# All of V' as rows in fp32r one period ahead, laid out anew through device memory

## The chip, the cores and the metric

One core of one Trainium2 chip runs the kernel. The metric is the device time of one execution in microseconds (us), the median of several. TensorE is called PE, VectorE DVE, ScalarE ACT, GpSimd POOL and SyncE SP, as the profile does.

## The reference

A block of cross attention and a quantised feed-forward layer over 128 samples of 64 positions and 128 features, with 16 heads:

```python
x = x + attention(layernorm(x), ctx_1024, ctx_1024, Wq, Wk, Wv, Wo, bo, mask)   # causal, dots * 64 ** -0.5
x = x + ffn(layernorm(x), w_gate, w_up, w_down)
# attention: softmax(q k^T) v over 16 heads of 64, then out @ Wo + bo
# ffn: bitlinear(silu(bitlinear(x, w_gate)) * bitlinear(x, w_up), w_down)
# bitlinear: activations rounded to 8 bits per row, weights to -1, 0, 1 times their mean size
```

## The kernel before

The samples go in 16 groups of eight, each group in two quads of four samples, so there are 32 quads. In the setup the kernel folds the weights: M = Wq Wk^T per head and N = Wv Wo per head, so that K' = ctx M and V' = ctx N come straight from the context, and the products of probabilities and V', summed over the heads, are the attention's output. A loop over 34 periods does in period n: the scores of quad n (`scores`, L411 for the later rows of the samples and L419 for the earlier ones), the product of quad n-1 (`attend`, L433 and L437, with V' in the tile `vp`), the transposes of the quantised x of quad n-1 (`transpose_xq`, L460), gate and up of quad n-1 (`gate_up`, L473, L476), down of quad n-2 (`down`, L446), and the transposes of the probabilities of quad n in three parts (`prob_transposes`, L489). A period with an even n also sums the next group's context on DVE (`sum_ctx`, L720), one with an odd n rounds and splits the one after it on ACT and POOL.

Between these stand units of work that depend on nothing late, each filling one PSUM bank of 128x512, four banks in turn: eight units of K' for the next group (`k_unit`, L294 to L296: three fp32r products of a high and a low part), four units of V' for the 32 later keys of each sample of quad n (`v_tiles`, L305: sixteen fp32 products into 32 partitions each, straight in the layout that `attend` wants, here called tile units), and four units of V' for the earlier keys of quad n+1 (`v_row_unit`, L313 to L315: three fp32r products with the samples' positions on all 128 partitions, here called row units). ACT copies every bank out (L540, with `take_v`, `take_key`, `take_rows`). The row units' copies lie in four tiles `v_rows` in a layout that `attend` can't use; SP moves each with four DMAs of 64 KB, 32 partitions to 32 partitions, into `vp` in the next period (`move_rows`, L235): 16 moves per quad.

The order on each engine is written out by hand, and semaphores are waited for at fixed counts. On PE a period reads: scores, attend, four tile units, four K' units, transposes of x, one K' unit, the late keys' mean (L454), down, gate and up, two K' units, probabilities' part 0, one K' unit, gate and up, part 1, four row units, part 2. DVE's order is: shift the scores by their bias (L779) and take row maxima, add the residual of quad n-1 and its statistics, quantise x (L840), then sum the exponentials and invert them (L801), then the feed-forward steps. POOL subtracts the row maxima (L978, L981), takes the roots (L922), and later multiplies the probabilities by the inverse sums (L990 in two halves, L992). The first half of L990 releases part 0 of `prob_transposes`.

Of the kernel before, what the change touches and what calls it, by code (L numbers as in the profile page):

```python
# [37 lines left out]
def build(nc, x, x_t, ctx_t, mask, wq, wk, wv, wo, bo, ffn_w, ident, causal, out):  # L42
# [14 lines left out]
    with ExitStack() as es:  # L57
# [21 lines left out]
        n_w = sb("n_w", [P, 2, HP, D])  # L79
# [30 lines left out]
        v_rows = [sb(f"v_rows{i}", [P, QB, D]) for i in range(QB)]  # L110
# [31 lines left out]

# [9 lines left out]
        m_ready, m_hi_done, m_lo_done, n_ready, n_done, n_hi_done, n_lo_done = (sem(n) for n in (  # L152
            "m_ready", "m_hi_done", "m_lo_done", "n_ready", "n_done", "n_hi_done", "n_lo_done"))
# [3 lines left out]
        k_ready, v_ready, scores_ready = (sem(n) for n in ("k_ready", "v_ready", "scores_ready"))  # L157
# [6 lines left out]
        vp_moved = [sem(f"vp_moved{i}") for i in range(QB)]  # L164

        cthi_ready, k_evac, v_evac, pt_evac, xqt_evac, exp_done, tanh_done = (sem(n) for n in (
            "cthi_ready", "k_evac", "v_evac", "pt_evac", "xqt_evac", "exp_done", "tanh_done"))
# [12 lines left out]
        V_UNITS, K_UNITS = QB, 8  # L180
# [3 lines left out]
        makes_k = lambda n: live(n) and n // 2 + 1 < GROUPS  # L184

# [6 lines left out]
        def _(sp):  # L192
# [25 lines left out]
            def load_ctx(g):  # L218

                sp.wait_ge(latesum_done, g - 1)  # L220
                sp.wait_ge(v_ready, V_UNITS * 2 * (g - 1))
                sp.dma_start(ct[g % 2][:], ctx_t[g]).then_inc(ctx_loaded[g % 2], 16)
# [6 lines left out]
            def move_rows(n, h4):  # L229

                if n:
                    sp.wait_ge(attn_ready, n)
                sp.wait_ge(rows_evac, QB * n + h4 + 1)
                for b in range(QB):
                    sp.dma_start(vp[h4 * R:(h4 + 1) * R, b, 0, :, :],  # L235
                                 v_rows[h4][b * R:(b + 1) * R, :, :]).then_inc(vp_moved[h4], 16)

            for n in PERIODS:
                g, r = n // 2, n % 2
                if live(n, 2):  # L240
                    for c in range(2):

                        sp.wait_ge(hb_ready, 2 * (n - 2) + c + 1)
                        if live(n, 3):
                            sp.wait_ge(down_ready, n - 2)
                        sp.dma_start_transpose(hid_t[:, c, :, :], hid_b[:, c, :]).then_inc(ht_moved, 16)
                if live(n):
                    move_rows(n, 0)
                    if r == 1 and g + 2 < GROUPS:
                        load_ctx(g + 2)  # L250
                    for h4 in range(1, QB):
                        move_rows(n, h4)
                if live(n) and r == 1 and g + 2 < GROUPS:
                    load_xt(g + 2)
                if live(n, 2):
                    store(n - 2)
                if makes_k(n) and r == 0:
                    if g:
                        sp.wait_ge(x1_done, 2 * g)
                    sp.dma_start(x_res[(g + 1) % 2][:], x[g + 1]).then_inc(xres_loaded[(g + 1) % 2], 16)  # L260
            for i in range(2):
                sp.wait_ge(stored[i], 16 * 2 * (GROUPS // 2))
# [3 lines left out]
        def _(pe):  # L266
# [34 lines left out]
            def v_tiles(n, b, dst):  # L301

                col = (n % 2 * 4 + 2) * P // 2 + b * R
                for h4 in range(QB):
                    t = mm(dst[h4 * R:(h4 + 1) * R, :], ct[n // 2 % 2][:, col:col + R], heads_of(n_w, h4),  # L305
                           start=True, stop=True)
                t.then_inc(v_ready, 1)

            def v_row_unit(n, h4, dst):

                par, cols = n // 2 % 2, slice(n % 2 * 2 * P, n % 2 * 2 * P + P)
                hi, lo = heads_of(n_hi, h4), heads_of(n_lo, h4)
# [40 lines left out]
            def fill_v(n, b):  # L353
                if not live(n):
                    return
                if b == 0:
                    pe.wait_ge(biased, 3 * n + 2)
                    pe.wait_ge(ctx_loaded[n // 2 % 2], 16 * (n // 4 + 1))
                elif b == 2:
                    pe.wait_ge(biased, 3 * n + 3)  # L360
                elif b == 3 and n:
                    pe.wait_ge(rows_evac, QB * n + 4)
                v_tiles(n, b, banks[b])

            def fill_k(n, u):
                if not makes_k(n):
                    return
                if u == 0 and n % 2 == 0:
                    pe.wait_ge(ctlo_ready, n // 2 + 2)
                if u < 4 and n == 0:  # L370
                    pe.wait_ge(rows_evac, u + 1)
                elif u < 4:
                    pe.wait_ge(v_evac, V_UNITS * n + u + 1)
                else:
                    pe.wait_ge(k_evac, H + K_UNITS * n + u - 3)
                k_unit(8 * (n % 2) + u, (n // 2 + 1) % 2, banks[u % 4])

            def fill_rows(n, h4):

                if not live(n):  # L380
                    return
                if n == 0:
                    pe.wait_ge(n_lo_done, h4 + 1)
                if n < 1:
                    pe.wait_ge(v_evac, h4 + 1)
                elif makes_k(n - 1):
                    pe.wait_ge(k_evac, H + K_UNITS * (n - 1) + h4 + 5)
                else:
                    pe.wait_ge(v_evac, V_UNITS * (n - 1) + h4 + 1)
                v_row_unit(n, h4, banks[h4])  # L390

            def scores(n):
# [4 lines left out]
                if n == 0:  # L397
                    pe.wait_ge(n_done, 4)
                else:
                    pe.wait_ge(rows_evac, QB * n + 2)  # L400
# [13 lines left out]
                if n:  # L414
                    pe.wait_ge(rows_evac, QB * n + 3)
# [7 lines left out]
            def attend(n):  # L423
                pe.wait_ge(pt_evac, 3 * n + 3)
                pe.wait_ge(v_evac, V_UNITS * n + V_UNITS)
                for h4 in range(QB):
                    pe.wait_ge(vp_moved[h4], 16 * QB * (n + 1))
# [64 lines left out]
            for n in PERIODS:  # L492
# [4 lines left out]
                fill_v(n, 0)  # L497
                fill_v(n, 1)
                fill_v(n, 2)
                fill_v(n, 3)  # L500
                if n == 0:
                    for h4 in range(QB):
                        fill_rows(0, h4)
                fill_k(n, 0)
                fill_k(n, 1)
                fill_k(n, 2)
                fill_k(n, 3)
# [4 lines left out]
                fill_k(n, 4)  # L512
# [26 lines left out]
        def _(act):  # L539
# [45 lines left out]
            def round_n(k):  # L585
                act.wait_ge(n_done, k + 1)
                part = slice(4 * (k // 2), 4 * (k // 2) + 4)
                copy(flat(n_hi[:, k % 2, part, :]), flat(n_w[:, k % 2, part, :])).then_inc(n_hi_done, 1)

            def take_v(n, b):  # L590
                if live(n):
                    act.wait_ge(v_ready, V_UNITS * n + b + 1)
                    if n:
                        act.wait_ge(attn_ready, n)
                    copy(flat(vp[:, b, 1, :, :]), banks[b]).then_inc(v_evac, 1)

            def take_key(n, u):
                if makes_k(n):
                    take_k((n // 2 + 1) % 2, 8 * (n % 2) + u, H + K_UNITS * n + u + 1, u % 4)

            def take_rows(n, h4):
                if live(n):
                    act.wait_ge(rows_ready, QB * n + h4 + 1)
                    if n:
                        act.wait_ge(vp_moved[h4], 16 * QB * n)
                    copy(flat(v_rows[h4][:, :, :]), banks[h4]).then_inc(rows_evac, 1)
# [18 lines left out]
            for n in PERIODS:  # L625
                if n == 0:
                    for k in range(4):
                        round_n(k)
# [3 lines left out]
                take_v(n, 0)  # L632
                take_v(n, 1)
                if live(n) and n:
                    exponential(n, 0)
                take_v(n, 2)
                if live(n) and n:
                    exponential(n, 1)
                take_v(n, 3)
                if n == 0:  # L640
                    for h4 in range(QB):
                        take_rows(0, h4)
                if n == 0:
                    exponential(n, 0)
                    exponential(n, 1)
                take_key(n, 0)
                take_key(n, 1)
                take_key(n, 2)
                take_key(n, 3)
# [4 lines left out]
                take_key(n, 4)  # L654
                if live(n, 1):
                    tanh(n - 1, 0)
                take_key(n, 5)
                take_key(n, 6)
                if live(n):
                    take_probs(n, 0)  # L660
                take_key(n, 7)
# [374 lines left out]
```

## Time and profile before

| | before |
|---|---|
| median of 3 runs | 706.51 us (704.72 to 708.13) |
| the profiled execution's own time | 707.55 us |
| its span in the trace | 705.7 us |
| mean granted clock of PE | 0.978 of full speed |
| busy, share of the span | PE 96%, DVE 76%, ACT 69%, POOL 50% |
| DMA engines, mean busy share of the data queue | 36.2% |
| moved by DMA | 63.31 MB, 72,922 packets |

The span is the part of the execution that the trace covers; the profiled execution took 1.85 us more than it. PE's matmuls are pipelined and their ends are modelled, so a row's length overlaps the next row; the distance from one start to another start is what a stretch of PE costs. In a timeline, several like instructions are merged into a row with their count (x8), and an idle time before a row stands in brackets with what ended it. Every fp32 product counts as two instructions in the trace.

### The profile page before, as it was taken

What the parts mean: (1) busy time and instruction counts of PE and PEld (TensorE: products, weight loads), DVE (VectorE), ACT (ScalarE), POOL (GpSimd) and SP (SyncE); (2) the same over time, 40 slices, a digit from 0 to 9 for tenths busy, and PEclk for the clock granted to TensorE, in tenths of its full rate; (3) what the DMA queues carried; (4) which work ended last, traced back from release to release, by engine and by line L of the source; (5) the groups of instructions that cost most, each with busy time, mean ns of one, the idle gap of its engine ahead of it and who ended that gap; (6) DMA issues with size and microseconds to landing.
All of it is one profiled execution on the core that took longest, in us unless ns stands there. A gap on an engine that the chain in (4) does not pass through costs nothing.

```text
span 705.7 us, 19010 instructions
## 1 busy us (share of the span) xinstructions
PE 675.8 (96%) x7258; PEld 452.9 (64%) x7258; DVE 535.7 (76%) x1398; ACT 487.6 (69%) x862; POOL 352.2 (50%) x359
## 2 busy tenths in 40 slices
PE   8999999999999999999999999999999999998852
PEld 5576766667766666676766667666666766665531
DVE  5667878778787877877878777787877777888663
ACT  5768767776886777678766767876676678665521
POOL 0536455464545546455554655555455545554531
PEclk9999999999999999999999999999999999999975
DMA  7023433333333434333433334353333434332231
GB/s 263 3 75 90 99 91 85 94 91 80 103 94 93 94 88 89 84 99 90 114 74 96 85 87 94 87 114 85 90 91 77 101 87 105 99 72 66 61 69 30
DMA packets 72922, 63.31 MB, mean 90 GB/s; under 512 B 44672, under 2 KB 49024, under 8 KB 72832
## 3 DMA queue, kind: packets, MB, share of 16 engines
q1 hardware_dynamic: 72832, 62.09, 36.2%
q8 instruction: 58, 0.95, 0.6%
q14 instruction: 32, 0.26, 0.1%
HBM read 15.91 MB, written 4.19 MB: 28 GB/s over the span
## 4 chain that ended last, share of the span: by engine, by line
PE 91%; issue 3%; POOL 2%; DVE 2%; DMA 1%; ACT 0%; POOLq 0%; SPq 0%; DVEq 0%
PE ps_up L411 8%; PE ps_up L305 7%; PE ps_a L433 7%; PE ps_b L489 6%; PE ps_up L294 5%; PE ps_up L295 4%; PE ps_up L296 4%; PE ps_low L305 4%; PE ps_kv L305 4%; PE ps_a L437 4%; PE ps_low L419 4%; PE ps_up L313 2%; PE ps_up L314 2%; PE ps_up L315 2%; PE ps_kv L294 2%
## 5 line engine op out<-in xcount | busy, mean ns | idle before, releaser
L540 ACT ACTIVATE vp<-ps_up 128x512 f32<-128x512 f32 x64 | 38.2, 597 | 143.1 <-PE ps_up L305 143.1
L990 POOL TENSOR_TENSOR prob_up<-prob_up,row_rec 128x512 f32<-128x512 f32 x64 | 65.9, 1051 | 129.6 <-DVE row_rec L801 129.6
L975 POOL TENSOR_TENSOR hid_b<-hid,neg_round 128x512 bf16<-128x512 f32 x64 | 65.2, 1039 | 105.9 <-ACT hid L540 105.9
L978 POOL TENSOR_TENSOR prob_up<-prob_up,row_max 128x1024 f32<-128x1024 f32 x32 | 61.2, 1913 | 62.7 <-DVE row_max L786 62.7
L848 DVE SCALAR_TENSOR_TENSOR gated<-gated,ps_g 128x512 f32<-128x512 f32 x64 | 44.0, 688 | 58.3 <-ACT gated L619 57.3
L779 DVE SCALAR_TENSOR_TENSOR prob_up<-ps_up,rs,bias_up 128x512 f32<-128x512 f32 x64 | 45.1, 748 | 48.4 <-PE ps_up L411 48.4
L540 ACT ACTIVATE kp<-ps_up 128x512 f32<-128x512 f32 x120 | 68.7, 605 | 8.9 <-PE ps_up L296 7.4
L433 PEld LDWEIGHTS ps_a<-vp,prob_t 128*32 128x32 f32 x2048 | 57.8, 111 | 19.7 <-issue 18.5
L433 PE MATMUL ps_a<-vp,prob_t 128*32 128x128 f32 x2048 | 62.6, 275 | 0.7 <-ACT prob_t L540 0.7
L540 ACT ACTIVATE prob_t<-ps_b 128x512 f32<-128x512 f32 x96 | 57.1, 594 | 7.7 <-PE ps_b L489 7.7
L411 PE MATMUL ps_up<-kp,xt 128*32 128x256 f32 (+1 forms) x768 | 61.9, 454 | 0.0
L305 PE MATMUL ps_up<-n_w,ct 128*32 128x512 f32 x512 | 60.8, 592 | 0.8 <-DVE prob_up L779 0.8
L294 PE MATMUL ps_up<-ct_hi,m_hi 128*128 128x512 f32 x120 | 58.7, 489 | 0.0
L922 POOL TENSOR_TENSOR rs<-ve,neg_half 128x2 f32<-128x2 f32 x64 | 44.4, 708 | 16.9 <-DVE ve L716 14.8
L619 ACT ACTIVATE gated<-ps_g,g_half 128x512 f32<-128x512 f32 x64 | 44.0, 687 | 11.6 <-PE ps_g L473 11.6
L295 PE MATMUL ps_up<-ct_lo,m_hi 128*128 128x512 f32 x120 | 47.5, 396 | 0.0
L296 PE MATMUL ps_up<-ct_hi,m_lo 128*128 128x512 f32 x120 | 47.5, 396 | 0.0
L853 DVE TENSOR_TENSOR hid<-gated,ps_u 128x512 f32<-128x512 f32 x64 | 44.0, 687 | 2.2
L540 ACT ACTIVATE hid<-hid,qs 128x512 f32<-128x512 f32 x64 | 42.7, 715 | 3.9 <-DVE qs L867 3.9
L489 PE MATMUL ps_b<-id_sb,prob_up 128*128 128x128 f32 x256 | 40.0, 280 | 4.1 <-POOL prob_up L990 3.8
L489 PEld LDWEIGHTS ps_b<-id_sb,prob_up 128*128 128x128 f32 x256 | 32.2, 143 | 16.9 <-POOL prob_up L990 5.9
L294 PEld LDWEIGHTS ps_up<-ct_hi,m_hi 128*128 128x128 f32 x120 | 22.6, 189 | 29.2 <-issue 24.3
(186 smaller groups left out, 1797.9 us busy)
## 6 DMA issues: line engine op xcount, KB each, us to landing
vp<-v_rows SPq DMA_DIRECT2D x512, 64.0 KB, 2.0
ct<-in_ctx_t SPq DMA_DIRECT2D x16, 256.0 KB, 2.8
x_res<-in_x SPq DMA_DIRECT2D x16, 256.0 KB, 2.8
xt<-in_x_t SPq DMA_DIRECT2D x16, 256.0 KB, 3.2
out<-x SPq DMA_DIRECT2D x32, 128.0 KB, 2.0
hid_t<-hid_b SPq DMA_TRANSPOSE x64, 2.7
kp<-in_wk SPq DMA_DIRECT2D x2, 256.0 KB, 3.7
kp<-in_wq SPq DMA_DIRECT2D x2, 256.0 KB, 4.4
```

The costliest lines, as they stand in the source:

```text
L294: mm(dst, hi, ct_hi[par][:], start=True, stop=False)
L295: mm(dst, hi, ct_lo[par][:], start=False, stop=False)
L296: mm(dst, lo, ct_hi[par][:], start=False, stop=True).then_inc(k_ready, 1)
L305: t = mm(dst[h4 * R:(h4 + 1) * R, :], ct[n // 2 % 2][:, col:col + R], heads_of(n_w, h4), start=True, stop=True)
L411: t = mm(ps_up[r * R:(r + 1) * R, col:col + w * R], xt[par][:, rows], kp[par][:, c * w:(c + 1) * w, key:key + R], start=True, stop=True)
L433: t = mm(ps_a[r * R:(r + 1) * R, 0:D], prob_t[:, a, r * R:(r + 1) * R], vp[:, r, a // QB, a % QB, :], start=(a == 0), stop=(a == HP - 1))
L489: t = nc.tensor.transpose(ps_b[:, k * P:(k + 1) * P], flat[:, k * P:(k + 1) * P], id_sb[:])
L540: copy = lambda dst, src, **kw: nc.scalar.activation(dst, src, ACT.Copy, **kw)
L779: v.scalar_tensor_tensor(prob_up[:, c, :, :], banks[c].rearrange("p (h j) -> p h j", j=R), rs1[:, 0:1], bias_up[:, n:n + 1, c * R:(c + 1) ...
L975: p.tensor_tensor(hid_b[:, c, :], hid[:, c, :], neg_round[:].broadcast_to([P, F]), ALU.add).then_inc(hb_ready, 1)
L978: p.tensor_tensor(prob_up[:], prob_up[:], row_max[0][:].rearrange("p (c h o) -> p c h o", c=1, o=1) .broadcast_to([P, 2, H, R]), ALU.subtr ...
L990: p.tensor_tensor(prob_up[:, half, :, :], prob_up[:, half, :, :], rows(row_rec[:, 0, :], H, R), ALU.mult).then_inc(normed, 1)
```

## The change

Nothing is left of the tile units: all of V' (both halves of the keys) is computed by row units, eight per quad, all in the period before the quad's own. N is then kept only as a high and a low part: ACT writes the high part from PSUM at once, and the low part is made by DVE from PSUM (`n_low`), where POOL made it from a copy (`split_n`). A device-memory tensor `v_mem` with room for two quads takes the rows: SP writes each of the eight `v_rows` tiles to it as one DMA of 256 KB (`save_row`), and in the quad's own period, after `attend` of the quad before, reads four pieces of 512 KB into `vp` (`load_v`), 32 partitions each, with 4 KB in a piece. `attend` waits for these four (`vp_loaded`). The table FILL sets in which of a period's 16 slots a row unit (o) or a K' unit (k) stands. Slots 0 to 6 come before the transposes of x, 7 after them, 8 and 9 before part 0 of the probabilities, 10 after it, and 11 to 15 between part 1 and part 2. Period 0 has eight more for quad 0.

```diff
-        n_w = sb("n_w", [P, 2, HP, D])
-        v_rows = [sb(f"v_rows{i}", [P, QB, D]) for i in range(QB)]
+        v_rows = [sb(f"v_rows{i}", [P, QB, D]) for i in range(2 * QB)]
...
+        FILL = "o0 o1 o2 o3 k0 k1 o4 k2 o5 k3 o6 k4 o7 k5 k6 k7"
+        FIRST_FILL = [("v", 0, u) for u in range(V_UNITS)]
+        def fills(n):
+            own = FIRST_FILL if n == 0 else []
+            if makes_k(n):
+                return own + [("kv"[c == "o"], n + (c == "o"), int(u)) for c, u in (w for w in FILL.split())]
+            return own + [("v", n + 1, u) for u in range(V_UNITS) if live(n + 1)]
...
-            def move_rows(n, h4):
+            def save_row(n, u):
+                jh, h4 = u // QB, u % QB
+                if n >= 2:
+                    sp.wait_ge(vp_loaded, 16 * QB * (n - 1))
+                sp.wait_ge(rows_evac, V_UNITS * n + u + 1)
+                sp.dma_start(v_mem[n % 2, h4, :, jh, :], v_rows[u][:, :, :].rearrange("p a e -> p (a e)")).then_inc(rows_saved[u], 16)
+            def load_v(n):
                 if n:
                     sp.wait_ge(attn_ready, n)
-                sp.wait_ge(rows_evac, QB * n + h4 + 1)
-                for b in range(QB):
-                    sp.dma_start(vp[h4 * R:(h4 + 1) * R, b, 0, :, :],
-                                 v_rows[h4][b * R:(b + 1) * R, :, :]).then_inc(vp_moved[h4], 16)
+                for h4 in range(QB):
+                    for jh in range(2):
+                        sp.wait_ge(rows_saved[jh * QB + h4], 16 * (n + 1))
+                    sp.dma_start(vp[h4 * R:(h4 + 1) * R, :, :, :, :].rearrange("p b c a e -> p b (c a e)"),
+                                 v_mem[n % 2, h4, :, :, :].rearrange("(b j) c x -> j b (c x)", j=R)).then_inc(vp_loaded, 16)
...
             def attend(n):
                 pe.wait_ge(pt_evac, 3 * n + 3)
-                pe.wait_ge(v_evac, V_UNITS * n + V_UNITS)
-                for h4 in range(QB):
-                    pe.wait_ge(vp_moved[h4], 16 * QB * (n + 1))
+                pe.wait_ge(vp_loaded, 16 * QB * (n + 1))
...
-                fill_v(n, 0)
-                fill_v(n, 1)
-                fill_v(n, 2)
-                fill_v(n, 3)
-                fill_k(n, 0)
-                fill_k(n, 1)
-                fill_k(n, 2)
-                fill_k(n, 3)
+                for i in range(0, 7):
+                    fill(n, i)
...
                     transpose_xq(n - 1)
-                fill_k(n, 4)
+                fill(n, 7)
...
-                fill_k(n, 5)
-                fill_k(n, 6)
+                for i in range(8, 10):
+                    fill(n, i)
                 if live(n):
                     prob_transposes(n, 0)
-                fill_k(n, 7)
+                fill(n, 10)
...
                     prob_transposes(n, 1)
-                fill_rows(n + 1, 0)
-                fill_rows(n + 1, 1)
-                fill_rows(n + 1, 2)
-                fill_rows(n + 1, 3)
+                for i in range(11, 16):
+                    fill(n, i)
                 if live(n):
                     prob_transposes(n, 2)
...
             def take_n(k):
-                copy(flat(n_w[:, k % 2, 4 * (k // 2):4 * (k // 2) + 4, :]), banks[N_BANK[k]]).then_inc(n_done, 1)
+                copy(flat(n_hi[:, k % 2, 4 * (k // 2):4 * (k // 2) + 4, :]), banks[N_BANK[k]]).then_inc(n_hi_done, 1)
...
+            def n_low(k):
+                dve.wait_ge(n_hi_done, k + 1)
+                half = slice(4 * (k // 2), 4 * (k // 2) + 4)
+                low_part(n_lo[:, k % 2, half, :], banks[N_BANK[k]], n_hi[:, k % 2, half, :], 1.0, n_lo_done)
```

The scores of quad 0 then wait for all four low parts (`n_lo_done`), since those read the banks that the scores overwrite.

PE in a period of the middle, just before and after the transposes of x (L460 before, L459 now). Before, the last K' unit ahead of them is the eighth unit after `attend`:

```order
L296 MATMUL ps_low<-ct_hi,m_lo 128x512
L294 MATMUL ps_kv<-ct_hi,m_hi 128x512
L295 MATMUL ps_kv<-ct_lo,m_hi 128x512
L296 MATMUL ps_kv<-ct_hi,m_lo 128x512
L460 MATMUL ps_a<-id_sb,xq 128x128 x2
L294 MATMUL ps_up<-ct_hi,m_hi 128x512
```

Now (row units at L332 to L334, K' units at L320 to L322):

```order
L332 MATMUL ps_low<-n_hi,ct_hi 128x512
L333 MATMUL ps_low<-n_hi,ct_lo 128x512
L334 MATMUL ps_low<-n_lo,ct_hi 128x512
L459 MATMUL ps_a<-id_sb,xq 128x128 x2
L320 MATMUL ps_kv<-ct_hi,m_hi 128x512
```

The unit for bank ps_kv, which stood ahead of the transposes, now stands behind them, and every later unit has moved back by one place: one more of them follows part 1 of the probabilities.

SP in two periods of the middle, an even one and the odd one after it. Before:

```order
L246 DMA_TRANSPOSE hid_t<-hid_b 128x4x128 x2
L235 DMA vp<-v_rows 32x512 x16
L227 DMA out<-x_0 128x256
L260 DMA x_res<-in_x 128x512
L246 DMA_TRANSPOSE hid_t<-hid_b 128x4x128 x2
L235 DMA vp<-v_rows 32x512 x4
L222 DMA ct<-in_ctx_t 128x512
L235 DMA vp<-v_rows 32x512 x12
L216 DMA xt<-in_x_t 128x512
L227 DMA out<-x_0 128x256
```

Now:

```order
L265 DMA_TRANSPOSE hid_t<-hid_b 128x4x128 x2
L254 DMA vp<-v_mem 32x4x1024 x4
L274 DMA x_res<-in_x 128x512
L232 DMA ct<-in_ctx_t 128x512
L245 DMA v_mem<-v_rows 128x512 x4
L237 DMA out<-x_0 128x256
L245 DMA v_mem<-v_rows 128x512 x4
L265 DMA_TRANSPOSE hid_t<-hid_b 128x4x128 x2
L254 DMA vp<-v_mem 32x4x1024 x4
L226 DMA xt<-in_x_t 128x512
```

The sixteen moves have become four reads, behind the same two transposes; the eight writes stand behind the reads and the inputs' loads, four ahead of the store of `out` and four behind it.

## Rows read from the trace of the kernel before

**Rows 1.** The page, part 1: busy time of each engine, share of the span, instructions.

```profile
PE 675.8 (96%) x7258; PEld 452.9 (64%) x7258; DVE 535.7 (76%) x1398; ACT 487.6 (69%) x862; POOL 352.2 (50%) x359
```

**Rows 2.** Waits: engine, tile, line, who was waited for: us in total, times, longest.

```profile
PE ps_a L460 <- DVE xq L840: 8.1, 3, 4.1
...
PE ps_b L489 <- POOL prob_up L990: 3.8, 2, 2.2
```

**Rows 3.** Timeline of PE, period 15: start us, us, engine, line, op, out<-in, forms.

```profile
332.73 1.92 PE L411 MATMUL ps_up<-kp,xt 128*32 128x512 f32 x16
...
337.95 1.90 PE L305 MATMUL ps_up<-n_w,ct 128*32 128x512 f32 x16
...
341.50 0.50 PE L294 MATMUL ps_up<-ct_hi,m_hi 128*128 128x512 f32 x1
...
344.39 0.38 PE L460 MATMUL ps_a<-id_sb,xq 128*128 128x128 f32 x2
...
347.81 0.60 PE L489 MATMUL ps_b<-id_sb,prob_up 128*128 128x128 f32 x4
...
350.54 0.39 PE L313 MATMUL ps_up<-n_hi,ct_hi 128*128 128x512 f32 x1
...
351.23 0.39 PE L313 MATMUL ps_low<-n_hi,ct_hi 128*128 128x512 f32 x1
...
353.13 1.93 PE L411 MATMUL ps_up<-kp,xt 128*32 128x256 f32 x32
```

**Rows 4.** Timeline of PE, period 16.

```profile
368.24 0.60 PE L489 MATMUL ps_b<-id_sb,prob_up 128*128 128x128 f32 x4
...
373.54 1.92 PE L411 MATMUL ps_up<-kp,xt 128*32 128x512 f32 x16
```

**Rows 5.** Timeline of DVE and POOL, period 15.

```profile
334.80 1.41 DVE L779 SCALAR_TENSOR_TENSOR prob_up<-ps_up,rs,bias_up 128x512 f32<-128x512 f32 x2 [1.24 <-PE ps_up L411]
...
338.08 1.91 POOL L978 TENSOR_TENSOR prob_up<-prob_up,row_max 128x1024 f32<-128x1024 f32 x1 [1.78 <-DVE row_max L786]
...
343.18 0.48 DVE L840 TENSOR_SCALAR xq<-xn,qs 128x128 f32<-128x128 f32 x2
...
345.82 0.35 DVE L801 RECIPROCAL row_rec<-row_sum 128x32 f32<-128x32 f32 x1
...
346.25 2.06 POOL L990 TENSOR_TENSOR prob_up<-prob_up,row_rec 128x512 f32<-128x512 f32 x2 [3.93 <-DVE row_rec L801]
```

**Rows 6.** Timeline of DVE and POOL, period 16.

```profile
364.13 0.41 DVE L720 TENSOR_REDUCE late_sum<-ct 128x8 f32<-128x256 f32 x1
...
367.00 2.06 POOL L990 TENSOR_TENSOR prob_up<-prob_up,row_rec 128x512 f32<-128x512 f32 x2 [4.25 <-DVE row_rec L801]
```

**Rows 7.** Timeline of PE and POOL, period 30, and the start of period 31.

```profile
638.84 1.93 PE L411 MATMUL ps_up<-kp,xt 128*32 128x256 f32 x32
...
652.38 2.05 POOL L990 TENSOR_TENSOR prob_up<-prob_up,row_rec 128x512 f32<-128x512 f32 x2 [3.92 <-DVE row_rec L801]
...
653.48 0.66 PE L489 MATMUL ps_b<-id_sb,prob_up 128*128 128x128 f32 x4 [2.20 <-POOL prob_up L990]
...
660.22 1.92 PE L411 MATMUL ps_up<-kp,xt 128*32 128x512 f32 x16
```

**Rows 8.** DMA issues: out<-in, queue, count, size, median us to landing.

```profile
vp<-v_rows SPq DMA_DIRECT2D x512, 64.0 KB, 2.0
```

**Rows 9.** Windows: stretch, us, busy us of engines, PEclk, DMA share, GB/s.

```profile
353.00:373.41 20.41, 20.41 (x234) 14.08 (x232) 16.16 (x44) 14.81 (x27) 10.29 (x11) 1.00 0.37 86
...
360.20:370.00 9.80, 9.80 (x66) 6.66 (x57) 7.83 (x25) 8.85 (x16) 5.55 (x7) 1.00 0.40 100
...
11.00:14.00 3.00, 2.81 (x23) 2.43 (x24) 1.06 (x3) 2.14 (x5) 0.00 (x0) 1.00 1.03 407
```

**Rows 10.** Timeline of ACT and PE at the end of the setup.

```profile
23.82 0.61 ACT L540 ACTIVATE n_w<-ps_up 128x512 f32<-128x512 f32 x1
...
24.84 2.17 PE L411 MATMUL ps_up<-kp,xt 128*32 128x256 f32 x32
```

More of the change, by code:

```diff
@@ L246, in _ @@
                         sp.dma_start_transpose(hid_t[:, c, :, :], hid_b[:, c, :]).then_inc(ht_moved, 16)
+                if n == 0:
+                    for u in range(V_UNITS):
+                        save_row(0, u)
                 if live(n):
[L248 to L256, printed above, removed]
+                    load_v(n)
                 if makes_k(n) and r == 0:
@@ L260, in _ @@
                     sp.dma_start(x_res[(g + 1) % 2][:], x[g + 1]).then_inc(xres_loaded[(g + 1) % 2], 16)
+                if r == 1 and g + 2 < GROUPS:
+                    load_xt(g + 2)
+                elif g + 2 < GROUPS:
+                    load_ctx(g + 2)
+                if live(n + 1):
+                    for u in range(4):
+                        save_row(n + 1, u)
+                if live(n, 2):
+                    store(n - 2)
+                if live(n + 1):
+                    for u in range(4, V_UNITS):
+                        save_row(n + 1, u)
             for i in range(2):
@@ L583, in take_n_sum, with take @@
                 copy(n_sum[:], ps_a[:, 0:D], scale=1.0 / (S * R)).then_inc(nsum_done, 1)
[L585 to L606, printed above, removed]
+            def take(n, i):
+                i += len(FIRST_FILL) if n == 0 else 0
+                if i >= len(fills(n)):
+                    return
+                kind, m, u = fills(n)[i]
+                if kind == "k":
+                    take_k((m // 2 + 1) % 2, 8 * (m % 2) + u, H + K_UNITS * m + u + 1, i % 4)
+                else:
+                    act.wait_ge(rows_ready, V_UNITS * m + u + 1)
+                    if m:
+                        act.wait_ge(rows_saved[u], 16 * m)
+                    copy(flat(v_rows[u][:, :, :]), banks[i % 4]).then_inc(rows_evac, 1)
             def round_hid(n, c):
@@ L653, in _ @@
                     take_xq(n - 1)
-                take_key(n, 4)
+                take(n, 7)
                 if live(n, 1):
                     tanh(n - 1, 0)
-                take_key(n, 5)
-                take_key(n, 6)
+                for i in range(8, 10):
+                    take(n, i)
                 if live(n):
                     take_probs(n, 0)
-                take_key(n, 7)
+                take(n, 10)
                 if live(n, 1):
@@ L665, in _ @@
                     take_probs(n, 1)
-                take_rows(n + 1, 0)
+                take(n, 11)
                 if live(n) and n % 2 == 1 and n // 2 + 2 < GROUPS:
                     round_ctx(n // 2 + 2)
-                take_rows(n + 1, 1)
-                take_rows(n + 1, 2)
-                take_rows(n + 1, 3)
+                for i in range(12, 16):
+                    take(n, i)
                 if live(n):
```

134 lines of the change are left out of this document (55 added, 79 removed).

## The prediction

> **What bounds the kernel now.** I read the busy times, the waits, then two periods of the timeline engine by engine. PE is busy 96% of the span [rows 1], and nearly all its waiting is in the first and last periods: three waits for x and two for the probabilities in the whole run [rows 2]. So a period of the middle costs what PE's own instructions cost: scores start at 332.73 and again at 353.13, 20.40 us later, and 20.41 us later again [rows 3, 4]. The reader might conclude that less work on PE is time saved one for one. That holds only as long as nothing PE waits for comes after PE would get there, so the second thing to read is how early those results are.
>
> The chain that matters starts with the scores themselves. DVE shifts them from 334.80, POOL subtracts the maxima from 338.08, DVE has quantised x by 343.18 + 0.48 = 343.66, has inverted the sums at 345.82 + 0.35, and POOL multiplies the probabilities from 346.25 in two halves of 1.03 [rows 5]. Part 0 can be transposed after the first half: at 347.28, which is 14.55 us after the scores' start. PE got there at 347.81, 15.08 after it [rows 3]. In an even period DVE also sums the context (0.41) in front of this, and POOL starts at 367.00 [rows 6]: ready 368.03, which is 14.90 after the start 353.13, and PE is there at 15.11 [rows 4]. **PE's slack at part 0 is thus 0.5 us in odd and 0.2 us in even periods.** It does not show as a wait, so the list of waits hides it. Period 30 makes no K' and shows the chain laid bare: POOL's first half ends at 652.38 + 1.03 = 653.41, PE starts at 653.48, 14.64 after its scores, and had idled 2.20 us [rows 7]. A result is used 0.08 us after POOL's recorded end.
>
> **The change, part by part.** *Units on PE.* From the first tile unit to the first K' unit it is 341.50 - 337.95 = 3.55 us for four; a row unit is 351.23 - 350.54 = 0.69, a K' unit 0.70 (four of them and a start after the tiled products make 344.39 - 341.50 = 2.89) [rows 3]. PE drops out of its tiled form once per period either way, about 0.2 us in all, now straight after `attend`. Ahead of the transposes stood 3.55 + 2.89 = 6.44 us; eight units in the new form would cost 0.2 + 8 x 0.70 = 5.8. PE's own work thus shrinks by **0.62 us per period**, 20 us in all, and this is the gain that the change seems to offer.
>
> *Where the units stand.* Only seven of them are now ahead of the transposes of x, and ten ahead of part 0 where there were eleven. The work ahead of part 0 falls by 0.62 + 0.70 = 1.32 us, and the work behind it rises by 0.70. Undisturbed, PE would reach the transposes of x at 11.66 - 1.32 = 10.34 us and part 0 at 15.08 - 1.32 = 13.76 (even: 13.79). But x is ready at 10.93 at the latest (343.66), so PE stops there for about 0.5 us, and part 0 is ready at 14.55, or 14.90, whatever PE does: every link of that chain hangs on the scores or on DVE's and POOL's fixed order, none on a unit. ACT's exponentials may start some 0.1 us earlier, since the two copies before them are of faster units, but DVE sums them only after quantising x, so nothing comes of it. With 0.08 of delay and about 0.04 for a cold start, part 0 begins at 14.67 in odd periods and at 15.02 in even ones. The first stop is swallowed by the second.
>
> *Per period.* From part 0 to the next scores it was 353.13 - 347.81 = 5.32 and 373.54 - 368.24 = 5.30 [rows 3, 4]; with one unit more it is 6.02 and 6.00. An odd period takes 14.67 + 6.02 = 20.69 (**+0.29**) and an even one 15.02 + 6.00 = 21.02 (**+0.61**). Periods 1 to 29: 15 x 0.29 + 14 x 0.61 = **+12.9 us**. What was saved stands as idle time ahead of part 0, and the moved unit is paid for in full.
>
> *Period 0 and the setup.* The last of N's copies starts at 23.82 and takes 0.61 [rows 10]; two low parts must follow on DVE, 1.41 / 2 = 0.70 each by the PSUM operation of the same shape [rows 5], so the scores start at about 25.9 instead of 24.84: +1.1. V' of quad 0 costs eight row units (5.7) for four tile and four row units (6.3): -0.6. Then three units more stand ahead of part 0 and one more behind: +2.8. Sum **+3.3**. POOL loses `split_n`, which only shortens a queue that isn't waited for here.
>
> *The tail.* Period 30 had four row units behind part 1; quad 31 now has its eight before part 0, in idle time. Period 30 took 660.22 - 638.84 = 21.38 [rows 7] and loses four units: **-2.8**. Period 31 loses its tile units, but it waits for the chain as period 30 did, and the rest is untouched: 0.
>
> *ACT and PSUM.* The copies stay 16 per period of the same shape, the banks go round as before: 0.
>
> *DMA.* A move lands 2.0 us after its issue [rows 8]. The reads are issued after `attend`, at about 6.4 us of the period behind the two transposes, and are wanted 2.6 us into the next: 17 us of cover. Their rate is not in the trace. Moves to 32 partitions ran at 100 GB/s with a share of 0.40, so 250 GB/s at full share; loads to all 128 partitions reached 407 [rows 9]. By these bounds 2.1 MB take 5.2 to 8.4 us, and the same for the eight writes. I take 8.4 for the reads (same 32 partitions as the moves) and 5.2 for the writes. The engines' load per period goes from 0.37 x 20.41 = 7.6 us, less 4.2 for the moves, plus 13.6, to 17.0 of about 20.9 us; with both at 250 GB/s it is 20.2. It fits, so this term is 0; it is also the term least known. On SP sixteen issues become twelve, and what a write waits for (its copy by ACT, the earlier reads) is done before SP reaches it; behind the last write stand the next period's transposes, which have until the down product, 12 us into it.
>
> The Trainium skill (SBUF — State Buffer, "Door 1: The DMA port swizzle") speaks against these reads: a transfer into 32 partitions reaches 8 of the 16 ports, some 218 GB/s, and two transfers to different partitions don't add up. By that, as an estimate from the page, the reads take 9.6 us, 1.2 more than by the moves' rate, and the sum stays. The moves' row agrees in kind, 250 against 407 GB/s, though a bit above the page's figure.
>
> *The sum.* 12.9 + 3.3 - 2.8 = +13.4 us on the profiled execution's 707.55, which gives 721.0. That execution lay 1.04 above the median of 706.51, so for the median I say **720 us**, 1.9% slower.
>
> **The rivals.** *The gain on PE is real (faster).* If the probabilities were ready before 13.8 us, PE would never stop, each period of the middle would fall by 0.62, and the time would be 706.5 - 29 x 0.62 + 0.5 = 689 us. For it: PE is at 96%, and POOL's recorded spans are rough. Against: in period 30 PE did wait, and began at 14.64, where POOL's row says. I give it 0.05. *Half way (no change).* If part 0 is ready 0.45 us before the rows say, the sum is nil: 706 us; about 0.07, for the same roughness. (0.5%, or 3.5 us, is about what a measurement of this kernel can tell.)
>
> *DMA becomes the bound (slower still).* The decisive point is a load of 20.9 us per period. If the reads run at 220 GB/s and the writes at 250 the load is 3.4 + 9.5 + 8.4 = 21.3, plus the end of one quad's writes that the next reads must wait for (2.0), which makes the chain read, attend, read longer than the rest: at a period of 21.7 the time is 720 + 29 x 0.8 = 743 us. For it: threefold traffic, in one queue. Against: 17 us of cover. 0.10. *The change does not do what it says*, that is, the row units run slower than 0.70 because the weights are the context: row units did so already, so no chance apart.
>
> **How the numbers follow.** The forecast of the chain gets 0.78; its own range, with 0.2 us per period of error either way and 2 us for setup and tail, is 712 to 730. The range reaches up towards DMA's case and a little below: 709 to 740. Faster by over 0.5%: 0.05; within: 0.07; slower: 0.78 + 0.10 = 0.88.
>
> **What would show it.** In the changed profile, PE's waits must name DVE's xq (near 0.5 us in each period) and POOL's prob_up (some 0.3 to 0.8 us in each) where there were three and two waits; periods alternate near 20.7 and 21.0; part 0 starts 14.7 and 15.0 us after the scores; five units stand behind part 1; no wait of `attend` for `vp`. I am wrong if part 0 starts earlier than 14.5 us, if PE waits for a DMA in each period, or if ACT's copies of the units hold PE back.

## The result, and the profile after

The changed kernel takes 722.37 us (median of four runs, 720.32 to 723.01) against 707.32 for the kernel before on the same chip (four runs: the three behind the 706.51 above and one more). The ratio is 1.0214, 95% interval 1.0179 to 1.0250: slower by 2.1%, where 720 us and 1.9% were forecast. The profiled execution's span grew from 705.7 to 720.8 us.

The page of the changed kernel, parts 1, 2 and 3 in part (the busy times answer to [rows 1]; in part 2 each digit is a fortieth of the span):

```profile
PE 668.6 (93%) x6586; PEld 490.1 (68%) x6618; DVE 531.8 (74%) x1402; ACT 483.6 (67%) x858; POOL 347.6 (48%) x355
...
PEclk9999999999999999999999999999999999999955
...
q1 hardware_dynamic: 103552, 162.75, 85.2%
```

PE is busy for less time, 668.6 us for 675.8, in a longer span. The data queue moves 162.75 MB where it moved 62.09, and its share has gone from 36.2% to 85.2%.

Who waited for whom in the changed kernel (total us, times, longest):

```profile
PEld ps_a L459 <- DVE xq L825: 33.2, 32, 5.9
PEld ps_b L488 <- POOL prob_up L967: 25.4, 32, 2.0
...
PE ps_a L459 <- DVE xq L825: 19.5, 29, 5.6
PEld ps_a L432 <- issue: 18.6, 62, 0.3
...
PE ps_b L488 <- POOL prob_up L967: 9.3, 17, 1.5
```

These are the two waits that [rows 2] had three times and twice; PE's own rows now have them 29 and 17 times. PE's weight loads (PEld) meet both in all 32 periods that have them, where they met them three and four times before. No wait of `attend` for `vp` is in the list. Such a wait could stand there as "issue", with nobody named; but at the lines of `attend` the weight loads have 18.6 us of it in 62 places, and had 18.5 in 62 before.

Part 4 of the two pages, the chain of work that ended last, says the same of the whole span. Before:

```profile
PE 91%; issue 3%; POOL 2%; DVE 2%; DMA 1%; ACT 0%; POOLq 0%; SPq 0%; DVEq 0%
```

and now:

```profile
PE 39%; POOL 23%; issue 21%; DVE 16%; ACT 1%; DMA 0%; POOLq 0%; DVEq 0%; SPq 0%
```

What took the time was PE's own work for 91% of the span, and is now for 39% of it; POOL and DVE have another 39%, and DMA 0%.

Timeline of the changed kernel, PE, periods 15 and 16, at the places of [rows 3, 4]:

```profile
342.39 1.92 PE L412 MATMUL ps_up<-kp,xt 128*32 128x512 f32 x16
...
353.20 0.52 PE L459 MATMUL ps_a<-id_sb,xq 128*128 128x128 f32 x2 [0.36 <-DVE xq L825]
...
357.04 0.66 PE L488 MATMUL ps_b<-id_sb,prob_up 128*128 128x128 f32 x4
...
358.68 0.60 PE L488 MATMUL ps_b<-id_sb,prob_up 128*128 128x128 f32 x4
...
362.62 0.60 PE L488 MATMUL ps_b<-id_sb,prob_low 128*128 128x128 f32 x4
...
363.15 1.93 PE L412 MATMUL ps_up<-kp,xt 128*32 128x256 f32 x32
...
378.13 0.66 PE L488 MATMUL ps_b<-id_sb,prob_up 128*128 128x128 f32 x4 [0.44 <-POOL prob_up L967]
...
384.24 1.06 PE L412 MATMUL ps_up<-kp,xt 128*32 128x512 f32 x8
```

and POOL at the same places:

```profile
355.93 2.06 POOL L967 TENSOR_TENSOR prob_up<-prob_up,row_rec 128x512 f32<-128x512 f32 x2 [3.93 <-DVE row_rec L786]
...
377.02 2.06 POOL L967 TENSOR_TENSOR prob_up<-prob_up,row_rec 128x512 f32<-128x512 f32 x2 [4.25 <-DVE row_rec L786]
```

The odd period takes 20.76 us, the even one 21.09; both took 20.4. Part 0 begins 357.04 - 342.39 = 14.65 and 378.13 - 363.15 = 14.98 us after the scores. POOL's first half of the probabilities ends at 355.93 + 1.03 = 356.96 and 378.05, 0.08 us before PE starts on it. In the odd period PE's row names no wait; the row of its weight load does:

```profile
357.04 0.42 PEld L488 LDWEIGHTS ps_b<-id_sb,prob_up 128*128 128x128 f32 x4 [0.55 <-POOL prob_up L967]
```

POOL's instruction stands 13.54 us after the odd scores, 13.52 before [rows 5]: the chain has not moved, PE has come up against it.

### The profile page after: what moved, and what is told of

The parts are those of the page before. It is cut to its first block, busy times and chain, and to the rows that moved or that the text cites. A ratio compares the mean times of both kernels' runs of the same rounds, so it can differ in the third digit from the quotient of the medians.

```text
span 720.8 us, 17711 instructions
## 1 busy us (share of the span) xinstructions
PE 668.6 (93%) x6586; PEld 490.1 (68%) x6618; DVE 531.8 (74%) x1402; ACT 483.6 (67%) x858; POOL 347.6 (48%) x355
## 3 DMA queue, kind: packets, MB, share of 16 engines
q1 hardware_dynamic: 103552, 162.75, 85.2%
## 4 chain that ended last, share of the span: by engine, by line
PE 39%; POOL 23%; issue 21%; DVE 16%; ACT 1%; DMA 0%; POOLq 0%; DVEq 0%; SPq 0%
POOL prob_up L955 8%; PE ps_up L412 8%; PE ps_b L488 7%; DVE prob_up L764 6%; POOL rs L907 6%; DVE row_max L771 5%; POOL prob_up L967 5%; POOL prob_low L958 4%; DVE prob_low L768 3%; PE ps_kv L322 2%; PE ps_kv L320 2%; PE ps_kv L321 2%; PE ps_up L332 1%; PE ps_up L333 1%; PE ps_up L334 1%
## 5 line engine op out<-in xcount | busy, mean ns | idle before, releaser
L531 ACT ACTIVATE v_rows<-ps_up 128x512 f32<-128x512 f32 x128 | 76.3, 598 | 148.5 <-PE ps_up L334 144.0
L432 PEld LDWEIGHTS ps_a<-vp,prob_t 128*32 128x32 f32 x2048 | 58.3, 112 | 19.9 <-issue 18.6
L531 ACT ACTIVATE kp<-ps_kv 128x512 f32<-128x512 f32 x90 | 53.8, 598 | 10.9 <-PE ps_kv L322 7.4
L332 PE MATMUL ps_up<-n_hi,ct_hi 128*128 128x512 f32 x128 | 59.3, 463 | 0.7 <-DVE prob_up L764 0.7
L531 ACT ACTIVATE v_rows<-ps_low 128x512 f32<-128x512 f32 x94 | 56.8, 604 | 3.3
L488 PEld LDWEIGHTS ps_b<-id_sb,prob_up 128*128 128x128 f32 x256 | 29.8, 143 | 32.4 <-POOL prob_up L967 25.4
L333 PE MATMUL ps_up<-n_hi,ct_lo 128*128 128x512 f32 x128 | 50.4, 394 | 0.0
L334 PE MATMUL ps_up<-n_lo,ct_hi 128*128 128x512 f32 x128 | 50.2, 392 | 0.0
L322 PE MATMUL ps_up<-ct_hi,m_lo 128*128 128x512 f32 x120 | 47.4, 395 | 0.0
```

What stands on the lines that cost most here:

```text
L322: mm(dst, lo, ct_hi[par][:], start=False, stop=True).then_inc(k_ready, 1)
L332: mm(dst, ct_hi[par][:, cols], hi, start=True, stop=False)
L432: t = mm(ps_a[r * R:(r + 1) * R, 0:D], prob_t[:, a, r * R:(r + 1) * R], vp[:, r, a // QB, a % QB, :], start=(a == 0), stop=(a == HP - 1))
L488: t = nc.tensor.transpose(ps_b[:, k * P:(k + 1) * P], flat[:, k * P:(k + 1) * P], id_sb[:])
L531: copy = lambda dst, src, **kw: nc.scalar.activation(dst, src, ACT.Copy, **kw)
```

## The experiments

Periods of the middle in the traces, with the places that matter (us after the scores; "behind" is from part 0 to the next scores):

| kernel | part 0, odd / even | behind | period, odd / even | median, us | against before (95%) |
|---|---|---|---|---|---|
| before | 15.08 / 15.11 | 5.3 | 20.40 / 20.41 | 706.3 to 707.8 | |
| the change | 14.65 / 14.98 | 6.1 | 20.76 / 21.09 | 722.37 | 1.0214 (1.0179 to 1.0250) |
| 1: before, a unit later | 14.64 / 14.97 | 6.1 | 20.71 / 21.02 | 721.5 | 1.0195 (1.0171 to 1.0219) |
| 2: change, 8 and 11 slots ahead | 14.65 / 14.99 | 5.4 | 20.06 / 20.40 | 703.07 | 0.996 (0.9941 to 0.9979) |
| 3: change, 8 and 12 slots ahead | 15.11 / 15.12 | 4.6 | 19.76 / 19.77 | 690.57 | 0.9767 (0.9748 to 0.9786) |
| 4: change, sum later | 14.64 / 14.65 | 6.1 | 20.75 / 20.76 | 717.72 | 1.0151 (1.0126 to 1.0176) |

**1. The order alone, in the kernel before.** Tile units and moves are as they were.

```diff
-                fill_k(n, 3)
...
                     transpose_xq(n - 1)
-                fill_k(n, 4)
+                fill_k(n, 3)
...
-                fill_k(n, 5)
-                fill_k(n, 6)
+                fill_k(n, 4)
+                fill_k(n, 5)
                 if live(n):
                     prob_transposes(n, 0)
-                fill_k(n, 7)
+                fill_k(n, 6)
...
                     prob_transposes(n, 1)
+                fill_k(n, 7)
                 fill_rows(n + 1, 0)
```

ACT's copies follow in the same order, here and in every run below.

> The kernel before, its tile units and its 16 moves untouched; only K' units stand one place later: three instead of four ahead of the transposes of x, one more behind part 1 of the probabilities. Theory A (the place of the units against the chain scores, DVE, POOL, part 0): PE reaches part 0 at 14.4 us and waits until 14.65 (odd) and 14.98 (even), the stretch behind it grows from 5.3 to 6.0; periods of 20.7 and 21.0, +0.3 and +0.65, some +14 us: 720 us, the whole slowdown of the change with none of its new V' and none of its device memory. Rival B (the slowdown comes from the traffic or from the new units): no difference, 706 to 708 us.

Measured 721.5 us, five runs. PE in its period 15:

```profile
339.61 1.92 PE L411 MATMUL ps_up<-kp,xt 128*32 128x512 f32 x16
...
354.25 0.66 PE L489 MATMUL ps_b<-id_sb,prob_up 128*128 128x128 f32 x4
...
360.32 1.93 PE L411 MATMUL ps_up<-kp,xt 128*32 128x256 f32 x32
```

Part 0 stands at 14.64, as in the changed kernel, and the period is 20.71. So putting K' units one place later, one more of them behind part 0, with no row unit more and no device memory, costs what the whole change costs. Rival B falls. The change's own gain on PE does not show in the comparison with the change, because there it only lengthens the idle time.

**2 and 3. The changed kernel, with slots moved forward.** In the second:

```diff
-                for i in range(0, 7):
+                for i in range(0, 8):
                     fill(n, i)
...
-                fill(n, 7)
+                for i in range(8, 9):
+                    fill(n, i)
...
-                for i in range(8, 10):
+                for i in range(9, 11):
                     fill(n, i)
                 if live(n):
                     prob_transposes(n, 0)
-                fill(n, 10)
+                for i in range(11, 12):
+                    fill(n, i)
...
-                for i in range(11, 16):
+                for i in range(12, 16):
```

The third has `range(9, 12)`, `range(12, 13)` and `range(13, 16)` in the last three places.

> The changed kernel with one unit moved forward: eight slots ahead of the transposes of x and eleven ahead of part 0, as many as before the change. Theory A: PE reaches part 0 at 14.5 us, waits for 14.65 and 14.98 still, and the stretch behind is 5.4: periods of 20.06 and 20.39, 0.70 less than the changed kernel's 20.76 and 21.09, 29 times: 702 us, some 0.6% under the kernel before. Rival B (DMA, which is busy 0.91 of a period, is the bound): the writes and reads cost 19.1 us plus their landings whatever the order, so little is gained: over 712 us.

> The changed kernel with eight slots ahead of the transposes of x, twelve ahead of part 0 and three behind part 1. Theory A: PE reaches part 0 at 15.15 us, after it is ready, and never waits; periods of 19.87 us, which is 20.41 less the 0.6 that the row units save: 691 to 692 us. Rival B (DMA): 19.1 us of transfers no longer fit into 19.9 us with the waits between reads, attend and writes; attend waits for vp and the period stays at 20.2 or more: 701 us or more.

Measured 703.07 us in 12 runs (expected 702; the runs spread from 701.85 to 707.10) and 690.57 in five (expected 691 to 692). PE in period 15 of the third:

```profile
327.61 1.92 PE L412 MATMUL ps_up<-kp,xt 128*32 128x512 f32 x16
...
342.72 0.60 PE L488 MATMUL ps_b<-id_sb,prob_up 128*128 128x128 f32 x4
...
344.30 0.60 PE L488 MATMUL ps_b<-id_sb,prob_up 128*128 128x128 f32 x4
...
346.84 0.60 PE L488 MATMUL ps_b<-id_sb,prob_low 128*128 128x128 f32 x4
...
347.37 1.93 PE L412 MATMUL ps_up<-kp,xt 128*32 128x256 f32 x32
```

and POOL ahead of it:

```profile
341.14 2.06 POOL L972 TENSOR_TENSOR prob_up<-prob_up,row_rec 128x512 f32<-128x512 f32 x2 [3.92 <-DVE row_rec L791]
```

POOL's half ends at 341.14 + 1.03 = 342.17, PE comes to it at 342.72 and finds it ready: part 0 begins at 15.11 with no wait. In the second experiment's even period 16, where a slot less lies ahead of it, the wait is there:

```profile
367.88 0.66 PE L488 MATMUL ps_b<-id_sb,prob_up 128*128 128x128 f32 x4 [0.40 <-POOL prob_up L972]
```

In the third experiment the period is 19.76: 0.64 less than before the change, which is the row units' saving, now on the clock. It beats the kernel before by 2.3%.

**4. One link out of the chain.** The sum over the next context goes behind `invert_sums` on DVE.

```diff
-                if makes_k(n) and n % 2 == 0:
-                    sum_ctx(n // 2 + 1)
                 if live(n):
                     sum_rows(n, 0)
                     sum_rows(n, 1)
                     invert_sums(n)
+                if makes_k(n) and n % 2 == 0:
+                    sum_ctx(n // 2 + 1)
```

> The changed kernel with the sum over the next group's context (0.41 us on DVE, even periods) put behind the inverse sums. Theory A: part 0 is ready in even periods when it is in odd ones, 14.65 us instead of 14.98, so even periods fall from 21.09 to 20.76: 14 times 0.33, 717.8 us. Rival B (DVE's order is not what part 0 waits for): no difference, 722 us.

Measured 717.72 us. In its even period 14 part 0 begins 335.26 - 320.61 = 14.65 after the scores:

```profile
320.61 1.93 PE L412 MATMUL ps_up<-kp,xt 128*32 128x256 f32 x32
...
335.26 0.66 PE L488 MATMUL ps_b<-id_sb,prob_up 128*128 128x128 f32 x4
...
341.37 1.92 PE L412 MATMUL ps_up<-kp,xt 128*32 128x512 f32 x16
```

What PE waits for is DVE's fixed order through POOL, as the theory has it.

**5. Without the reads.** It leaves out the reads of V' for quads 2 to 31 (63 MB), so `attend` works on quad 1's V' from then on; this changes the result and not the work on any engine but DMA.

```diff
-                if live(n):
+                if n < 2:
                     load_v(n)
...
-                    sp.wait_ge(vp_loaded, 16 * QB * (n - 1))
+                    sp.wait_ge(vp_loaded, 16 * QB * min(n - 1, 2))
...
-                pe.wait_ge(vp_loaded, 16 * QB * (n + 1))
+                pe.wait_ge(vp_loaded, 16 * QB * min(n + 1, 2))
```

> The changed kernel, but device memory is read into vp in periods 0 and 1 only: it leaves out 30 of the 32 quads' reads (15.7 of 16.8 MB of each four), so attend uses quad 1's V' ever after. Theory A: the transfers are wholly hidden in the changed kernel, part 0 still waits for POOL: 722 us. Rival B (the reads' traffic slows something, a share of the 0.07 us by which each period exceeded the prediction): 715 to 720 us.

(The bytes in that text are wrong; 30 quads of 2.1 MB are left out.) Measured 722.02 us, four runs within 0.2; the ratio to the kernel before is 1.0215, where the change has 1.0214. Leaving the reads out gives nothing: they are hidden entirely in the changed kernel.

**6. The third and the fourth together** (edits as above).

> The third experiment (twelve slots ahead of part 0) with the fourth's later sum over the context. Theory A: PE reaches part 0 at 15.11, after it is ready at 14.98, so making it ready at 14.65 is worth nothing here, where it was worth 4.6 us in the changed kernel: 690 to 691 us. Rival F (DVE's order saves the same 4 to 5 us wherever it stands): 686 us.

Measured 689.39 us, ratio 0.9754 (0.9723 to 0.9785), whose interval holds the third's ratio. Most middle periods are 19.76 and 19.77 as in the third; what was worth 4.6 us where PE waited is worth nothing in the middle where it does not. The 1.2 us between the medians can't be told from no difference here.

**7 and 10. Is it the order alone?** The kernel before, with its last K' unit ahead of part 0:

```diff
+                fill_k(n, 7)
                 if live(n):
                     prob_transposes(n, 0)
-                fill_k(n, 7)
```

> The kernel before with one K' unit put ahead of part 0 (twelve instead of eleven) and none between part 0 and gate. Theory A: PE never waited there, so the order can't give anything: periods of 20.4, 706 us; what the third experiment gained is the row units' 0.6 us per period, set free by the order. Rival B (the order alone gives it, by the 0.2 to 0.5 us of slack): 695 us.

Measured 722.81 us, which neither theory nor rival expected. Both missed a second wait. PE at the place, period 15:

```profile
356.84 0.60 PE L489 MATMUL ps_b<-id_sb,prob_up 128*128 128x128 f32 x4
...
358.27 0.63 PE L489 MATMUL ps_b<-id_sb,prob_up 128*128 128x128 f32 x4 [0.40 <-ACT prob_t L540]
```

and ACT, which must copy part 0 out of the bank first:

```profile
357.54 0.59 ACT L540 ACTIVATE prob_t<-ps_b 128x512 f32<-128x512 f32 x1
```

Parts 0 and 1 share one PSUM bank. With gate and up alone between them, PE stands still until ACT's copy ends at 358.13. It came without a wait when a unit lay there: 1.59 us from part to part, of which 0.70 was the unit. Taking it away left 1.43, so 0.54 us of the unit's time was not work saved but cover lost. The period is 20.97 instead of 20.40. The tenth run keeps a unit in that gap (the first row unit moves up into it):

```diff
+                fill_k(n, 7)
                 if live(n):
                     prob_transposes(n, 0)
-                fill_k(n, 7)
+                fill_rows(n + 1, 0)
...
                     prob_transposes(n, 1)
-                fill_rows(n + 1, 0)
                 fill_rows(n + 1, 1)
```

> The kernel before with twelve units ahead of part 0 (the last K' unit moved there), and the first row unit put into the gap between part 0 and gate, so that one unit of cover stays between parts 0 and 1, where the seventh experiment had taken it away. Theory A, mended (the seventh run was slow because part 1 waited for ACT's copy of part 0, not because twelve units ahead are bad): no wait anywhere, periods of 20.4, as the kernel before: 706 to 708 us. Rival E (a unit more ahead of part 0 costs 0.6 us per period by itself): 722 us again.

Measured 705.67 us in ten runs, ratio 0.9985 (0.9965 to 1.0004), periods 20.41 and 20.43. The order of the third experiment gives nothing with the tile units. Its 2.3% come from the row units in that order.

**8 and 9. How near DMA is.** To the third experiment come two, or four, more writes of 256 KB per period.

```diff
+                if u in (0, 4):
+                    sp.dma_start(v_spare[n % 2, h4, :, jh, :], v_rows[u][:, :, :].rearrange("p a e -> p (a e)")).then_inc(rows_saved[u], 16)
```

(with (0, 2, 4, 6) in the ninth, and the counts of `rows_saved` doubled for these).

> The fastest kernel so far (eight slots ahead of x, twelve ahead of part 0) with two of the eight writes done twice, the second time to a spare tensor: 0.5 MB or 1.3 us more per period at the 400 GB/s that its writes reach. Its queue is busy 96.5% of the span and no engine waits for it. Theory C (one queue in order, 19.3 us of transfers in a period of 19.77): the queue now needs 20.6 us, attend waits for vp, periods of 20.6: 715 us. Rival D (the share overstates the load, as its sum grew from 614 to 665 us at equal bytes): the extra writes fit or nearly fit, 691 to 700 us.

> The same with four of the eight writes done twice: 1 MB or 2.6 us more per period. Theory C: 21.9 us per period, some 750 us, and twice the step of the run with two. Rival D: about 1 us of slack is used up first, periods of 20.8 to 21.2: 720 to 733 us.

Measured 708.63 us (+18.1 over the third, ratio to the kernel before 1.0027, 1.0009 to 1.0044) and 743.4 us (+52.8, ratio 1.0527, 1.0491 to 1.0564). In the traces the middle, from the scores of period 1 to those of period 30, took 573.6 us in the third and takes 16.7 and 51.1 more. The second step is 34.8 us by the medians and 34.4 in the 29 periods of these traces, about 1.2 us per period for 0.5 MB; the first is half of it, 0.6. If the first 0.5 MB cost as much as the second, about 0.6 us was still free in the third experiment's 19.77, and the queue needs some 19.2 us per period. That is an estimate, and a mean: in the eighth, periods 13, 14 and 16 still take 19.76 to 19.79 us and period 10 takes 21.37. Theory C's price, 1.3 us, is a little high, and it misses that slack; rival D's 691 to 700 us and 720 to 733 us are both too low.

PE waits in two places. The waits of the eighth:

```profile
PE ps_b L447 <- DMA hid_t<-hid_b: 14.5, 7, 9.2
...
PE ps_a L434 <- issue: 4.8, 7, 1.0
...
PE ps_a L438 <- issue: 2.6, 3, 0.9
```

of the ninth:

```profile
PE ps_b L447 <- DMA hid_t<-hid_b: 42.9, 27, 9.2
...
PE ps_a L434 <- issue: 11.4, 11, 3.3
```

and of the third, without added writes:

```profile
PE ps_b L445 <- DMA hid_t<-hid_b: 9.2, 1, 9.2
```

The one long wait of 9.2 us is the last down product of the run, and every kernel here has it, the kernel before too. What the added writes brought at the down product is the rest: 5.3 us in six places, then 33.7 in 26. It waits for its transposes, which stand in the queue behind the writes. The other place is `attend`, with 4.8 and 11.4 us, where theory C put the wait. The trace names no releaser there, but the times fit `vp`. In period 17 of the eighth:

```profile
376.24 1.95 PE L434 MATMUL ps_a<-vp,prob_t 128*32 128x128 f32 x64 [0.98 <-issue]
```

The reads for it (tile `vp`, window 350 to 380) were issued from 361.8 to 363.7:

```profile
L256 SPq DMA_DIRECT2D vp<-v_mem x4: 302/310/319, 361.8 to 363.7; - x4
...
DMA to landing us min/median/max: 5.6/8.4/12.5
```

If the longest of these landings is the last read's, it ends at 363.7 + 12.5 = 376.2, where `attend` starts. The 2.6 us at L438 are something else: they lie inside the product, where the kernel waits for nothing, in periods 12, 20 and 28, and no run shows what holds PE there.

## Why the prediction was right, point by point

**The slack that no wait shows.** Right. PE's slack of 0.5 and 0.2 us at part 0, read from POOL's rows, set the result (0.45 and 0.13 when the 0.08 us from POOL's end to PE's start are taken off). Part 0 was put at 14.67 and 15.02 and stands at 14.65 and 14.98. Runs 1 to 4 show it from three sides: the order makes it, more cover unmakes it, and DVE's 0.41 us moves it.

**The row unit's saving.** 0.62 us per period was worked out, 0.64 measured in the third run (20.41 - 19.77), hidden in the changed kernel as forecast. PE's busy time is a poor measure of it: it fell by 7.2 us in the changed kernel, where 20 us of work were forecast to go, and by 21.1 in the third experiment (654.7), because a row's modelled end runs on into an idle time behind it (L322 in the changed kernel stands at 356.53 for 0.39 us, though these rows follow each other every 0.23).

**Behind part 0.** This term was a little small: 6.02 and 6.00 were forecast, 6.11 measured in both. Between parts 0 and 1 it is 358.68 - 357.04 = 1.64 where it was 1.59, the transposes after an idle time being slower (0.66 for 0.60, I had put 0.04 for it ahead of part 0 instead; it is 1.58 in the third experiment, where no idle time lies ahead), and between parts 1 and 2 it is 3.94, where 3.20 and a unit of 0.70 make 3.90. Periods of 20.76 and 21.09 for 20.69 and 21.02 are some 2 us in 29. Period 1 was priced like the other odd ones, but before the change it has no down product and took 20.00 us, and now takes 20.75; period 3 takes 21.00, for a reason that is open. Together the middle, from the scores of period 1 to those of period 30, grew by 15.4 us (606.86 for 591.42), not 12.9.

**Setup and period 0.** 3.3 us were forecast, 1.8 measured. Period 0 itself grew by 24.25 - 22.58 = 1.67, not 2.2; why it is less is open. The first scores started only 0.15 us later (24.99 for 24.84), not 1.1. The wait for the low parts was there (0.80 us on DVE's `n_lo`), but that execution's setup ran 0.7 us ahead on PE: its last K' unit started at 23.33, where it was 24.05 before. This is scatter. In the four traces of kernels with tile units the first scores start at 24.50 to 25.37, in the eight with row units at 24.99 to 26.27; the means, 24.89 and 25.77, lie 0.9 apart, near the 1.1 of the forecast.

**The tail.** Period 30 lost 3.3 us (18.04 for 21.38), a little more than the 2.8, and what follows gained 1.2 where 0 was forecast. PE idles 5.64 us in period 31 ahead of the transposes of x (1.96 before), the granted clock over the last two slices is 5 and 5 tenths where it was 7 and 5 (5 is the lower of its two levels, 1.2 GHz), and the first part of the product of quad 31 takes 3.36 us for 2.79 (timeline of the changed kernel, PE):

```profile
694.55 3.36 PE L432 MATMUL ps_a<-vp,prob_t 128*32 128x128 f32 x64 [0.69 <-ACT prob_t L531]
```

That the change causes the 1.2 us is not shown. From the scores of period 31 to the end, the four traces with tile units take 43.6 to 47.4 us (the kernel before 45.5), and the six with row units and no added writes 44.7 to 46.7 (the changed kernel 46.7).

So 1.8 + 15.4 - 3.3 + 1.2 = 15.1 us, the difference of the spans, where 3.3 + 12.9 - 2.8 + 0 = 13.4 was forecast. The terms were off by -1.5, +2.5, -0.5 and +1.2, which partly cancel; that the sum came as near as 1.7 us is in part luck. The mechanism does not hang on it: the periods and the place of part 0 came out to within 0.1 us.

**DMA.** That it hides was right (run 5 takes away the reads, and run 1, as slow, moves nothing of V' through device memory), the load was not. I put 17.0 of 20.9 us; by the share of the two periods in this table it is 0.96 x 20.76 and 0.87 x 21.09, 19.1 on average (columns as in [rows 9]):

```profile
342.39:363.15 20.76, 20.23 (x196) 14.66 (x196) 15.81 (x43) 15.03 (x28) 11.71 (x12) 1.00 0.96 257
363.15:384.24 21.09, 20.25 (x213) 15.19 (x213) 16.16 (x44) 14.73 (x27) 10.06 (x10) 1.00 0.87 230
```

Reads alone and writes alone:

```profile
353.40:359.40 6.00, 5.83 (x37) 4.43 (x38) 4.35 (x10) 4.83 (x10) 3.47 (x4) 1.00 1.02 211
359.60:363.30 3.70, 3.70 (x22) 2.89 (x24) 3.43 (x8) 3.59 (x8) 1.74 (x3) 1.00 1.05 398
```

The writes go at 398 GB/s, the 5.2 us that I took. The reads go at 211, not at the moves' 250, and take 10 us rather than 8.4. The Trainium skill (SBUF — State Buffer, "Door 1: The DMA port swizzle") has 218 GB/s for 32 partitions, and the trace of the change agrees with it better than the row I had preferred. In the changed kernel this cost nothing. The rival's decisive point was well placed: at 19.2 us of transfers the changed kernel had 1.7 us of room, and experiments 8 and 9, whose periods would be 19.8 us without waits, go past theirs.

The rivals of the faster side (0.05 and 0.07) fell because PE started 0.08 us after POOL's recorded end in each period read here, so these ends can be relied on to within 0.1 us, rough as POOL's spans were held to be.

## What to carry to other kernels

A busy engine without waits may be fractions of a microsecond short of one. Before work is taken out ahead of a wait, or moved behind it, compare the time at which the awaited result ends with the time at which the engine gets there; only what exceeds that slack is lost, and the place of the filler decides whether a cheaper instruction shows at all. Moving a filler has two ends: the place it goes to and the wait it covered where it was (experiment 7); and after every gain ask which queue is next, here DMA with some 0.6 us to spare.

## What the runs showed of the hardware that was not expected

The data queue's share is not a load that can be added up. For the same 162.75 MB it was 85.2% of 720.8 us, 614 us, in the changed kernel and 96.5% of 689.3, 665 us, in the third experiment. A window of 1 us in the third experiment reads 3.04 of full at 145 GB/s, while the writes of the changed kernel moved 398 GB/s at 1.05:

```profile
531.00:532.00 1.00, 1.00 (x6) 0.82 (x5) 0.97 (x5) 0.39 (x1) 1.00 (x1) 1.00 3.04 145
```

Part 3 of the third experiment's page:

```profile
q1 hardware_dynamic: 103552, 162.75, 96.5%
```

At 96.5% there was still some 0.6 us of room per period, by the estimate of experiments 8 and 9. What the second pair of extra writes cost, about 1.2 us per 0.5 MB, is the better measure.

A transfer's time to landing says little in a full queue. Part 6 of the changed kernel's page (KB each, median us from issue to landing):

```profile
v_mem<-v_rows SPq DMA_DIRECT2D x256, 256.0 KB, 9.8
vp<-v_mem SPq DMA_DIRECT2D x128, 512.0 KB, 8.0
```

The writes landed 9.8 us after their issue (median) and the reads 8.0, where the moves took 2.0 [rows 8], and no engine waited for any of them.
